# A transformer block on one core: an Exp bias in place of a matmul row, an earlier projection, and the expert tables in one pass

## The chip, the core and the metric

The kernel runs on 1 core of a Trainium2 chip. TensorE (PE) multiplies, ScalarE (ACT) applies functions, VectorE (DVE) and GpSimd (POOL) do elementwise work, and SP only issues DMAs. Each engine has its own queue and executes it in order; they meet at semaphores. The metric is the device time of one execution in microseconds (us), lower is better.

## The reference

Two layers on x of shape (2, 1024, 256), each behind a layer norm without scale and with a residual add: attention, then a mixture of experts.

```python
x = x + attention(_layernorm(x), wq, wk, wv, wo)
x = x + ffn(_layernorm(x), w_router, wg, wu, wd, sg, su, sd)
# attention: 32 heads of 8 dims, 8 key/value heads
scores = einsum('bhqd,bhkd->bhqk', q, k) / sqrt(8)
amask  = where((j >= i - 128) & (j < i), -1e10, 0)   # a band below the diagonal is masked
out    = einsum('bhqk,bhkd->bqhd', softmax(scores + amask), v) @ wo
# ffn: 8 routed experts, the top 2 per token with normalized sigmoid weights, and 2 shared ones
out = sum_e comb[t, e] * (silu(xt @ wg[e].T) * (xt @ wu[e].T)) @ wd[e].T + shared experts
```

## The kernel before, in words

**The start** (PE's L1557 to L1590). x comes in as 4 chunks of 512 rows. DVE takes each row's statistics, ACT the root, DVE the normalized rows; PE turns them (`transpose_x`, L1535), ACT copies the turned halves to `x1T` (`xT1_out`, L849), PE projects to q, k and v. PE passes the time up to the first turn with idle transposes (`idle_turns`, L1542: 52, later 8). q and k are split into three bf16 parts (`parts`), go to DRAM and come back, laid one above the other, as `qst` and `kst` of the stack of a group (`load_stack`, L527 and L530, SP). Rows of constants and shifts lie in the same stacks, so that one matmul adds up all the products. A bound on the scores, from the largest norms, is computed on a 1x1 chain of DVE and ACT; its negative is spread by a 1-column matmul (L1590) to 128 partitions and written as the row `kst[0]` and `kst[64]` by DVE (L1106) and ACT (L907), so that each score comes out with the bound subtracted. If the bound is too large for that, a flag starts an exact pass over all scores; all engines load the flag and branch (PE at L1594). With these inputs the flag is 0.

**The attention loop.** 16 groups (2 batches x 8 key/value heads), each 29 Exps over score blocks of 128 keys x 1024 (queries and heads), one of them of 512. PE computes scores (`scores`, L1616) into three double banks, DVE merges the masked diagonal blocks (`merge_pair`, L1149), ACT takes Exp (L930, L941, L933) into `prob`, POOL masks (`mask_pair`, L759), PE sums values and denominators in units of 4 heads (`values`, L1663) into banks 6 and 7. The order on PE is written out by hand in `TURNS`, 14 turns of products and ended values. Meanwhile DVE splits the expert weights, and SP loads the next stacks. DVE copies the sums out (`acc_out`, L1137), SP stores them to `o_scr`. PE may start a stack only when the semaphore `st_in` has its count; a first share of 32 is added by SP itself (L545).

**Out of the loop.** The sums of a chunk of 512 rows are loaded (`load_sums`), DVE inverts the denominators (`invert`, 4 pieces) and multiplies (`normalize`), PE projects with wo (`project`, L1716), DVE adds to x (`new_rows`, L1221), takes the second layer norm (`layernorm`, L449 to L462, root on ACT), PE turns (`transpose_rows`, L1726), ACT copies to `x2T` (`x2_out`, L947), and DVE takes the low parts and a plain copy (`xT_copy`) for the router. For chunk 0 all this stands behind the loop, for chunks 1 to 3 between the steps of the shared experts.

**The shared experts.** 4 chunks of 10 steps: `shared_up` (L1765, 12 matmuls), silu on ACT, products on DVE, `shared_down` (L1778). Routing is computed on DVE between steps 24 to 37 (`routing`): `slot_rows`, `slot_values` and `place_rows` make one-hot tables, PE multiplies them (`slot_products`, L1752), which gives for each slot of the 40 routed tiles its token and weight, and `slot_table` makes index lists of them.

**The routed experts.** Up to 40 tiles of 128 slots. POOL gathers rows (`gather`, L799) and adds results to `out` (`add`, L809); its adds wait until SP has stored the rows of the shared part, the last of them behind the load of expert 1. DVE's scaled result (`y_out`, L1506) waits for a free buffer that POOL's add gives back (L814).

## Time and profile before

| | us |
|---|---|
| median of 3 runs | 952.74 |
| lowest, highest | 952.62, 954.16 |
| the profiled execution | 952.9 |
| its span | 951.2 |
| TensorE's mean granted clock in it | 0.983 of full |

Busy in the span: PE 896.4 us (94%), ACT 583.4 (61%), DVE 444.9 (47%), POOL 278.7 (29%). These are means over stages that differ: the start to about 57 us, the attention loop to about 494, the shared experts to about 709, the routed ones to the end. A stage has to be read by itself, by stretches and by the timeline.

### The profile page before, as it was taken

The page shows a single profiled execution, that of the slowest core. Times are in us where ns is not written, and L with a number is a line of the kernel's source. Part 1 is how long each engine was busy: PE and PEld are TensorE (multiplying, and loading weights), DVE is VectorE, ACT ScalarE, POOL GpSimd, SP SyncE. Part 2 cuts the span into 40 slices and gives each one's busy share as a digit, 9 for nine tenths or more (in the row PEclk, how much of TensorE's full clock was granted, in tenths as well). Part 3 has the DMA queues.
Part 4 walks back from the last instruction along what each step waited for, and adds up shares of the span by engine and source line. Part 5 has one row for each costly group of instructions (what it writes and reads, how often), then busy time and mean ns, then how long its engine had stood idle before and what let it go on. Part 6 is the DMA issues. An engine that isn't in the chain of part 4 may idle for free.

```text
span 951.2 us, 24249 instructions
## 1 busy us (share of the span) xinstructions
PE 896.4 (94%) x8221; PEld 570.8 (60%) x8222; DVE 444.9 (47%) x761; ACT 583.4 (61%) x733; POOL 278.7 (29%) x422
## 2 busy tenths in 40 slices
PE   9959999999999999999988999999999999999994
PEld 6513333333333333333346888888887888888883
DVE  7724433444444334444456777656653433434332
ACT  4769999999999999999972423332222222222221
POOL 4403333233233333333330000000012545445442
PEclk9969999999999999999997999999999999999998
DMA  5433445555544455532202207100027864564521
GB/s 178 130 112 103 162 157 206 206 199 196 175 149 159 154 206 206 204 93 90 55 22 66 67 18 238 45 1 23 1 81 256 265 209 98 156 180 127 150 35 22
DMA packets 41951, 123.67 MB, mean 130 GB/s; under 512 B 7608, under 2 KB 22968, under 8 KB 35760
## 3 DMA queue, kind: packets, MB, share of 16 engines
q1 hardware_dynamic: 31152, 110.35, 34.0%
q0 software_dynamic: 7008, 9.70, 5.7%
q10 hardware_dynamic: 3744, 3.02, 1.0%
q8 instruction: 25, 0.41, 0.2%
q14 instruction: 22, 0.18, 0.1%
HBM read 74.03 MB, written 49.02 MB: 129 GB/s over the span
## 4 chain that ended last, share of the span: by engine, by line
PE 78%; ACT 8%; DVE 6%; issue 5%; SPq 1%; DMA 1%; DVEq 0%; POOLq 0%; POOL 0%; ACTq 0%
PE ps L1663 18%; PE ps L1811 14%; PE ps L1616 13%; PE ps L1765 11%; ACT arena L930 7%; PE ps L1830 7%; PE ps L1778 5%; DVE ps L1149 3%; PE ps L1557 2%; PE ps L1821 2%; PE ps L1716 1%; PE ps L1542 1%; PE ps L1792 1%; PE ps L1752 1%; PE ps L1734 1%
## 5 line engine op out<-in xcount | busy, mean ns | idle before, releaser
L930 ACT ACTIVATE arena<-ps 128x1024 f32<-128x1024 f32 x336 | 317.0, 1044 | 6.9 <-PE ps L1616 6.9
L1663 PE MATMUL ps<-arena 128*32 128x256 f32 x4096 | 265.1, 385 | 0.1
L759 POOL TENSOR_SCALAR_AFFINE_SELECT arena<-arena 128x512 f32<-128x512 f32 x240 | 150.0, 638 | 302.3 <-ACT arena L941 203.1
L1616 PE MATMUL ps<-arena 64*128 64x512 bf16 (+1 forms) x1280 | 184.5, 343 | 21.5 <-SPq L545 7.7
L1663 PEld LDWEIGHTS ps<-arena 128*32 128x32 f32 x4096 | 111.8, 109 | 103.1 <-issue 38.2
L1149 DVE COPY_PREDICATED ps<-keep,ps 128x512 f32<-128x512 int32 (+1 forms) x128 | 80.5, 629 | 172.1 <-PE ps L1616 172.1
L1616 PEld LDWEIGHTS ps<-arena 64*128 64x128 bf16 x1280 | 53.7, 94 | 175.4 <-ACT arena L930 82.2
L1811 PE MATMUL ps<-wr_all,x2T 128*128 x648 | 144.9, 364 | 5.7 <-issue 3.6
L1811 PEld LDWEIGHTS ps<-wr_all,x2T 128*128 128x128 f32 x648 | 105.6, 189 | 28.0 <-issue 13.7
L1765 PE MATMUL ps<-x2T,wr_all 128*128 128x512 f32 x480 | 118.8, 399 | 1.2 <-issue 1.2
L941 ACT ACTIVATE arena<-ps 128x1024 f32<-128x1024 f32 x112 | 114.2, 1034 | 8.0 <-DVE ps L1149 3.6
L1765 PEld LDWEIGHTS ps<-x2T,wr_all 128*128 128x128 f32 x480 | 89.5, 192 | 19.1 <-issue 1.6
L978 ACT CAST x2T<-ps 128x640 fp32r<-128x640 f32 x36 | 25.0, 693 | 107.4 <-PE ps L1821 101.4
L791 POOL COPY now_from<-slot_from 128x1 int32 (+1 forms) x36 | 10.1, 281 | 246.7 <-issue 232.0
L956 ACT ACTIVATE arena<-ps 128x512 f32<-128x512 f32 x40 | 23.9, 597 | 83.4 <-PE ps L1765 83.2
L1830 PE MATMUL ps<-wr_all,x2T 128*128 x540 | 73.3, 288 | 1.7 <-DVE x2T L1498 1.7
L809 POOL DMA_INDIRECT out<-arena,now_to x36 | 57.2, 1589 | 58.6 <-issue 46.9
L1830 PEld LDWEIGHTS ps<-wr_all,x2T 128*128 128x128 f32 x540 | 66.8, 191 | 2.1 <-issue 2.1
L983 ACT ACTIVATE arena<-ps 128x640 f32<-128x640 f32 x36 | 25.3, 704 | 64.1 <-PE ps L1811 62.3
L1778 PE MATMUL ps<-wr_all,hsh 128*128 128x256 f32 x480 | 64.1, 285 | 0.2 <-DVE hsh L1267 0.2
L1778 PEld LDWEIGHTS ps<-wr_all,hsh 128*128 128x128 f32 x480 | 61.8, 191 | 2.9 <-DVE hsh L1267 0.6
L1156 DVE CAST wr_all<-raw 128x1280 fp32r<-128x1280 f32 x30 | 24.7, 824 | 69.8 <-POOL arena L759 69.8
(187 smaller groups left out, 731.6 us busy)
## 6 DMA issues: line engine op xcount, KB each, us to landing
w_scr<-wr_all SPq DMA_DIRECT2D x24, 1280.0 KB, 7.0
wr_all<-w_scr SPq DMA_DIRECT2D x24, 1280.0 KB, 5.6
raw<-w_experts SPq DMA_DIRECT2D x24, 640.0 KB, 7.1
arena<-q_scr SPq DMA_DIRECT2D x64, 64.0 KB
o_scr<-arena SPq DMA_DIRECT2D x128, 32.0 KB, 1.6
arena<-o_scr SPq DMA_DIRECT2D x16, 256.0 KB, 3.9
raw<-w_shared SPq DMA_DIRECT2D x6, 640.0 KB, 4.2
q_scr<-parts SPq DMA_DIRECT2D x8, 384.0 KB, 2.8
```

Of the source, the lines that this page charges most:

```text
L759: nc.gpsimd.affine_select(out=dst, in_=src, compare_op=ALU.is_ge if own else ALU.is_gt, fill=0.0, base=0, pattern=[[0, REP], [-1 if own el ...
L809: nc.gpsimd.indirect_dma_start(out=out, in_=ysb[:, p, :], in_offset=None, compute_op=ALU.add, out_offset=bass.IndirectOffsetOnAxis(ap=now_ ...
L930: nc.scalar.activation(prob[:, SLOT[unit(a, kt)], :, :].rearrange("p h q -> p (h q)"), score.rearrange("p b x -> p (b x)"), ACT.Exp, scale ...
L941: nc.scalar.activation(halves, score.rearrange("p b (h s q) -> p (b h) s q", h=2, s=2), ACT.Exp, scale=SCALE).then_inc(s_free, 1)
L983: nc.scalar.activation(gact[:, p, :], ps[:, 0:3, :].rearrange("p b n -> p (b n)")[:, 0:I], ACT.Silu) \
L1149: nc.vector.copy_predicated(into, mask, source).then_inc(merged, 1)
L1616: return nc.tensor.matmul(ps[:, bank, :].rearrange("p (h q) -> p h q", h=2)[:, :, place * P:(place + tiles) * P], kst[r0:r0 + HALF, s, kt ...
L1663: last = nc.tensor.matmul(ps[32 * h:32 * h + 32, 6 + qc, a % 2 * QW:(a % 2 + 1) * QW], vst[:, s, kt, :], prob[:, SLOT[k], h, :], start=(no ...
L1765: last = nc.tensor.matmul(ps[:, 2 * (q % 2) + half, :], wr_all[:, q // KI, k, w, o:o + P], x2T[:, v, k, ds(c * CT, CT)], start=(k == 0 and ...
L1778: last = nc.tensor.matmul(ps[:, 4 + t // 2, t % 2 * D:(t % 2 + 1) * D], hsh[:, q % HR, v, t * P:(t + 1) * P], wr_all[:, q // KI, 2, w, o:o ...
L1811: last = nc.tensor.matmul(ps[:, n0 // 512, 0:n], xsT[:, p, v, k, :], wr_all[:, ds(slot, 1), k, w, n0:n0 + n].rearrange("p o n -> p (o n)") ...
L1830: last = nc.tensor.matmul(ps[:, 6, 0:D], hidT[:, p, v, k, :], wr_all[:, ds(slot, 1), 2, w, k * D:(k + 1) * D].rearrange("p o n -> p (o n)" ...
```

## The change

- The bound is copied by ACT to a [128, 1] tile `bound` and given to all Exps as bias. The rows `kst[0]` and `kst[64]` stay constant, those of `qst` zero; both memsets move from DVE to POOL. The four copies at L1106 and L907 go. `st_in`'s first share is added at the beginning of SP's program.
- The start: 30 and 4 idle turns for 52 and 8, and the second half of chunk 0's `x1T` is copied by DVE.
- Chunk 0's chain is moved into the loop: its sums are loaded after group 10, three of the four inversions stand in groups 12 to 14, the fourth and the product in group 15. `project(0)` stands in two halves between the last scores, into banks that are free by then (`FIRST_O`), and the last nine units of values behind it. Adds and statistics follow on DVE (`add_first`, `first_rows`), the turned rows go to banks 4 and 5 (`XT_BANK`).
- The tables: all operands are rounded fp32r, so that a product is one pass. The weight goes in as two parts, 3 x 40 = 120 columns for 2 x 40. The one-hot positions lie over columns of `x2T` that chunks 0 and 1 have used. The passes stand in steps 36 and 37 for 35 and 37, `place_rows(1)` in step 35 for 36.

The diff, cut to its core:

```diff
-EXP_STEP, RANK_STEP, TABLE_STEPS = 23, 27, (35, 37)
+EXP_STEP, RANK_STEP, TABLE_STEPS = 23, 27, (36, 37)
+HOT = 3
...
             sp.sem_inc(w_split, 2)
+            for s in range(2):
+                sp.sem_inc(st_in[s], 32)
...
             load_stack(1, 1)
-            for s in range(2):
-                sp.sem_inc(st_in[s], 32)
...
-            sp.wait_ge(o_stored[0], 16 * REP * KV + FIRST)
-            load_sums(0)
-            group_io(NG - 1, 1, False, False, False)
-            for c in range(1, NC):
+            for n in range(2 * LOOPED, NG - 1):
+                group_io(n, n % 2, n < SPLIT_PAIRS, n + 1 < NG - 1, n + 2 < NG)
+                if n == 2 * LOOPED:
+                    sp.wait_ge(o_stored[0], 16 * REP * KV + FIRST)
+                    load_sums(0)
+            store_acc(NG - 1, 0)
+            sp.wait_ge(o_stored[1], 16 * REP * KV + FIRST)
+            sp.wait_ge(c_proj, 2 + FIRST)
+            load_sums(1)
+            store_acc(NG - 1, 1)
+            for c in range(2, NC):
...
-                for k in range(KD):
+                for k in range(KD if c else 1):
                     nc.scalar.copy(x1T[:, c % 2, k, :], ps[:, k, :]).then_inc(a_xT, 1)
...
-            for s in range(2):
-                nc.scalar.copy(kst[HALF:HALF + 1, s, :], ps[HALF:HALF + 1, 7, 128:129].to_broadcast([1, L])) \
-                    .then_inc(shift_high, 1)
+            nc.scalar.copy(bound, ps[:, 7, 128:129]).then_inc(bound_ready, 1)
+            act.wait_ge(bound_ready, 1)
...
                         nc.scalar.activation(prob[:, SLOT[unit(a, kt)], :, :].rearrange("p h q -> p (h q)"),
-                                             score.rearrange("p b x -> p (b x)"), ACT.Exp, scale=SCALE).then_inc(s_free, 1)
+                                             score.rearrange("p b x -> p (b x)"), ACT.Exp, bias=bound, scale=SCALE).then_inc(s_free, 1)
...
+            def add_first(half):
+
+                dve.wait_ge(c_proj, half + 1 + FIRST)
+                for t in range(2 * half, 2 * half + 2):
+                    nc.vector.tensor_tensor(x_rows(0, t), x_rows(0, t), ps[:, FIRST_O[half], t % 2 * D:(t % 2 + 1) * D],
+                                            ALU.add) \
+                        .then_inc(c_added, 1)
+                for t in range(2 * half, 2 * half + 2):
+                    dve.wait_ge(c_added, t + 1)
+                    nc.vector.bn_stats(stats[:, t, :], x_rows(0, t)).then_inc(dve_step, 1)
...
             merge_pair(NG - 1, 1)
-            invert(0, 0)
-            invert(0, 1)
+            invert(0, INVERT - 1)
+            normalize(0)
             merge_pair(NG - 1, 2)
             acc_out(NG - 1, 0)
             merge_pair(NG - 1, 3)
-            invert(0, 2)
-            invert(0, 3)
-            normalize(0)
+            add_first(0)
+            add_first(1)
+            first_rows()
             acc_out(NG - 1, 1)
-            new_rows(0)
             xT_copy(0)
...
-                link(nc.vector.tensor_tensor(hot[:, :, 0, :], hot[:, :, 1, :], over_tiles(token_less_T[:, :], NTILE), ALU.mult))
-                nc.vector.tensor_tensor(hot[:, :, 1, :], hot[:, :, 1, :], over_tiles(w, NTILE), ALU.mult).then_inc(r_hot, 1)
+                nc.vector.tensor_tensor(hot[:, :, 0, :], one, over_tiles(token_less_T[:, :], NTILE), ALU.mult)
+                link(nc.vector.tensor_tensor(hot[:, :, 2, :], one, over_tiles(w_parts[:, k, 1, :].bitcast(F32), NTILE), ALU.mult))
+                nc.vector.tensor_tensor(hot[:, :, 1, :], one, over_tiles(w_parts[:, k, 0, :].bitcast(F32), NTILE), ALU.mult) \
+                    .then_inc(r_hot, 1)
...
-            idle_turns(7, 52)
+            idle_turns(7, 30)
             transpose_x(0)
-            idle_turns(7, 8)
+            idle_turns(7, 4)
...
+            products_of(*last, LAST_MERGE + 2, False)
+            pe.wait_ge(c_oT, 1)
+            pe.wait_ge(merged, NG * NMERGE)
+            project(0, range(0, 2))
+            products_of(*last, LAST_MERGE + 3, False)
+            pe.wait_ge(s_free, NG * NEXP - 2 + BUFS)
+            project(0, range(2, 4))
...
-                    last = nc.tensor.matmul(ps[:, 6, 0:2 * NTILE], pos_hot[k][:, t, :],
+                    last = nc.tensor.matmul(ps[:, 6, 0:HOT * NTILE], pos_hot[k][:, t // TPC, t % TPC, :],
...
-            project(0)
+            pe.wait_ge(s_free, NG * NEXP + BUFS)
             transpose_rows(0)
```

The order on two engines, at the two places that matter most. First ACT between the end of the start and the first Exps of the loop; before, with `ps` the scores and `arena` the memory in which `kst`, `prob` and the 1x1 values lie:

```order
L901 ACTIVATE arena<-arena 1x1 [waits u_top]
L904 ACT_TABLE_LOAD [waits ones_ready]
L904 ACTIVATE exp_of_one<-arena 1x1 [waits const]
L907 CAST arena<-ps 1x1024 [waits u_shift]
L907 CAST arena<-ps 1x1024
L930 ACTIVATE arena<-ps 128x1024 [waits s_ready,p_free] x7
L941 ACTIVATE arena<-ps 128x4x2x128 [waits merged,p_free]
```

and after:

```order
L913 ACTIVATE arena<-arena 1x1 [waits u_top]
L916 ACT_TABLE_LOAD [waits ones_ready]
L916 ACTIVATE exp_of_one<-arena 1x1 [waits const]
L918 COPY arena<-ps 128x1 [waits u_shift]
L941 ACTIVATE arena<-ps,arena 128x1024 [waits bound_ready,s_ready,p_free]
L941 ACTIVATE arena<-ps,arena 128x1024 [waits s_ready,p_free] x6
L952 ACTIVATE arena<-ps,arena 128x4x2x128 [waits merged,p_free]
L944 ACTIVATE arena<-ps,arena 128x4x128 [waits s_ready,p_free]
```

The two copies of 1x1024 have become one of 128x1, and each Exp (now L941, L952, L944) reads `arena` beside `ps`: the [128, 1] bound.

Then PE from the last scores to the turning of chunk 0's rows (L1616, now L1647, are scores; L1663, now L1694, values; L1716, now L1742, the projection; L1726, now L1772, the turns). Before, with the first of the six units of values that stand in between:

```order
L1616 MATMUL ps<-arena 128x512 [waits s_free]
L1616 MATMUL ps<-arena 128x512
L1663 MATMUL ps<-arena 32x256 [waits s_free]
L1663 MATMUL ps<-arena 32x256 x3
...
L1716 MATMUL ps<-wo_sb,arena 128x256 [waits c_lsb,c_oT,acc_free]
L1716 MATMUL ps<-wo_sb,arena 128x256 x3
L1716 MATMUL ps<-wo_sb,arena 128x256 [waits acc_free]
L1716 MATMUL ps<-wo_sb,arena 128x256 x3
L1726 MATMUL ps<-ident,arena 128x128 [waits c_xn]
L1726 MATMUL ps<-ident,arena 128x128 x7
```

and after, without the last eight units:

```order
L1647 MATMUL ps<-arena 128x512 [waits s_free]
L1647 MATMUL ps<-arena 128x512
L1742 MATMUL ps<-wo_sb,arena 128x256 [waits merged,c_oT]
L1742 MATMUL ps<-wo_sb,arena 128x256 x3
L1647 MATMUL ps<-arena 128x512 [waits s_free]
L1647 MATMUL ps<-arena 128x512
L1742 MATMUL ps<-wo_sb,arena 128x256 [waits s_free]
L1742 MATMUL ps<-wo_sb,arena 128x256 x3
L1694 MATMUL ps<-arena 32x256 [waits masked,s_free]
L1694 MATMUL ps<-arena 32x256 x3
...
L1772 MATMUL ps<-ident,arena 128x128 [waits c_xn,s_free]
L1772 MATMUL ps<-ident,arena 128x128 x7
```

The projection has moved ahead of the last scores and of the last nine units of values, half of it behind the third-last Exp, and the turns come straight after the values.

## Rows read from the trace of the kernel before

**Rows 1.** Stretches, two groups of the loop: busy us (instructions) per engine, clock, DMA

```profile
195.00:249.00 54.00, 52.33 (x672) 20.50 (x668) 21.86 (x30) 52.93 (x59) 18.65 (x30) 1.00 0.52 182
```

**Rows 2.** Costliest groups, the Exps: count | busy us, mean ns | idle before, releaser

```profile
L930 ACT ACTIVATE arena<-ps 128x1024 f32<-128x1024 f32 x336 | 317.0, 1044 | 6.9 <-PE ps L1616 6.9
L941 ACT ACTIVATE arena<-ps 128x1024 f32<-128x1024 f32 x112 | 114.2, 1034 | 8.0 <-DVE ps L1149 3.6 <-PE ps L1663 1.0
```

**Rows 3.** Timeline, twelve Exps in a row on ACT: start, us, what

```profile
217.33 11.24 ACT L930 ACTIVATE arena<-ps 128x1024 f32<-128x1024 f32 x12
```

**Rows 4.** Groups by shape on DVE, the last one on ACT: with and without [128,1] operands

```profile
L1506 DVE TENSOR_SCALAR arena<-ps,slot_w 128x256 f32<-128x256 f32 x36 | 17.4, 484 | 21.0 <-POOLq L814 11.1 <-issue 4.8 <-PE ps L1830 2.9
...
L1275 DVE TENSOR_TENSOR xres<-xres,ps 128x256 f32<-128x256 f32 x16 | 5.7, 416 | 4.0 <-PE ps L1778 4.0
...
L1034 DVE TENSOR_SCALAR arena<-xres,meanvar,rstd 128x256 f32<-128x256 f32 x16 | 5.6, 414 | 0.1
...
L1131 DVE COPY arena<-arena 128x256 f32 x10 | 2.9, 287 | 0.0
...
L1027 DVE TENSOR_SCALAR rstd<-meanvar 128x4 f32<-128x4 f32 x4 | 0.7, 170 | 0.1
...
L844 ACT ACTIVATE rstd<-rstd 128x4 f32<-128x4 f32 x8 | 1.7, 207 | 17.7 <-DVE rstd L456 16.0 <-DVE rstd L1027 1.6
```

**Rows 5.** Timeline, DVE: four and two of these in a row

```profile
12.39 1.38 DVE L1034 TENSOR_SCALAR arena<-xres,meanvar,rstd 128x256 f32<-128x256 f32 x4
...
52.06 0.47 DVE L1131 COPY arena<-arena 128x256 f32<-128x256 f32 x2
```

**Rows 6.** Timeline of the start; the last row is of the DMA issues (us to landing)

```profile
3.56 0.57 ACTq L891 DMA_DIRECT2D wr_sb<-w_router  x1
...
9.89 1.04 PE L1535 MATMUL ps<-ident,arena 128*128 128x128 f32 x8
...
12.30 5.53 PE L1557 MATMUL ps<-arena 128*128 128x512 f32 x12 [0.50 <-ACT arena L849]
...
wr_sb<-w_router ACTq DMA_DIRECT2D x1, 8.0 KB, 7.4
```

**Rows 7.** PE's branch on the flag (ns, start us); timeline, its first scores

```profile
L1594 PEldq COMPARE_BRANCH  x1: 365/365/365, 50.3 to 50.3; - x1
...
57.49 1.47 PE L1616 MATMUL ps<-arena 64*128 64x512 bf16 x6 [7.74 <-SPq L545]
```

**Rows 8.** Timeline out of the loop; the last row is a stretch with its clock

```profile
489.80 2.88 ACT L930 ACTIVATE arena<-ps 128x1024 f32<-128x1024 f32 x3
...
491.31 2.87 PE L1663 MATMUL ps<-arena 128*32 128x256 f32 x48
...
494.11 3.72 PE L1716 MATMUL ps<-wo_sb,arena 128*128 128x256 f32 x16
...
498.80 1.41 DVE L449 BATCH_NORM_STATS2 stats<-xres 128x6 f32<-128x256 f32 x4 [0.17 <-DVE xres L1221]
...
502.66 1.97 PE L1726 MATMUL ps<-ident,arena 128*128 128x128 f32 x8 [4.83 <-DVE arena L462]
...
505.84 5.46 PE L1765 MATMUL ps<-x2T,wr_all 128*128 128x512 f32 x12 [1.21 <-issue]
...
520.22 2.91 PE L1765 MATMUL ps<-x2T,wr_all 128*128 128x512 f32 x12
...
508.00:510.00 2.00, 2.00 (x6) 1.52 (x6) 1.86 (x2) 0.00 (x0) 0.00 (x0) 0.50 0.00 0
```

**Rows 9.** Timeline, tables and first weighed result; the last row is a DVE group

```profile
679.19 3.77 PE L1752 MATMUL ps<-arena,xres 128*128 128x80 f32 x32 [1.68 <-issue]
...
687.84 0.69 DVE L1264 TENSOR_TENSOR arena<-arena,ps 128x512 f32<-128x512 f32 x1 [3.61 <-ACT arena L956]
...
730.94 0.48 DVE L1506 TENSOR_SCALAR arena<-ps,slot_w 128x256 f32<-128x256 f32 x1 [2.93 <-POOLq L814]
...
L1427 DVE TENSOR_TENSOR arena<-arena,per_t 128x640 f32<-128x640 f32 x2 | 1.7, 826 | 0.1
```

More of the change, by code:

```diff
@@ L1170, in split_part, with group @@
                     split(n, p, lambda p: (w_staged[:, p, 0, :], w_staged[:, p, 1, :]), None)
-            def group(g, s, more):
+            def group(g, s, more, also=lambda: None):
                 merge_pair(g, 1)
+                also()
                 merge_pair(g, 2)
@@ L1193, in _ @@
                     group(it * 2 + s, s, True)
-            for n in range(2 * LOOPED, NG - 1):
-                group(n, n % 2, n + 2 < NG)
             def x_rows(c, t):
@@ L1666, in values, with products_of @@
                 last.then_inc(p_free, 1)
-            def turn_of(n, s, turn, t, before, after):
-                products, ended = TURNS[t]
-                for p in products:
+            def products_of(n, s, turn, t, after):
+                for p in TURNS[t][0]:
                     if not isinstance(p, int):
@@ L1720, in project @@
                         last.then_inc(c_proj, 1)
+            LAST_MERGE = max(t for t, (products, _) in enumerate(TURNS) if (QP - 1, 1) in products)
+            last = (NG - 1, 1, NG // 2 - 1)
+            for t in range(1, LAST_MERGE + 2):
+                turn_of(*last, t, True, False)
+            products_of(*last, LAST_MERGE + 2, False)
[5 more added lines that the diff above has]
+            project(0, range(2, 4))
+            for t in range(LAST_MERGE + 2, len(TURNS)):
+                if t > LAST_MERGE + 3:
+                    products_of(*last, t, False)
+                values_of(*last, t, True)
+            for v in TURNS[0][1]:
+                if len(v) == 3:
+                    values(NG - 1, 1, unit(*v[0:2]))
             def transpose_rows(c):
                 pe.wait_ge(c_xn, c + 1)
+                rows = xnc if c else xnc_first
                 for k in range(KD):
                     for t in range(TPC):
-                        last = nc.tensor.transpose(ps[:, 6 + k, t * P:(t + 1) * P], xnc[:, t, k * P:(k + 1) * P],
+                        last = nc.tensor.transpose(ps[:, XT_BANK[c] + k, t * P:(t + 1) * P], rows[:, t, k * P:(k + 1) * P],
                                                    ident[:, :])
```

143 lines of the change are left out of this document (74 added, 69 removed).

## The prediction

> **What bounds the kernel now.** I read the table of stretches first. In the attention loop, here two of its 16 groups, ACT is busy 52.93 of 54 us and PE 52.33 [rows 1]. Both look full, but PE's ends are modelled. The costliest groups of instructions tell them apart: the loop is 336 + 112 Exps of 1024 columns, of about 1.04 us each, and 16 of half that length [rows 2]. Twelve in a row take 11.24 us, so one starts every (11.24 - 1.04) / 11 = 0.927 us [rows 3]. A group has 29 Exps and takes 27.1 us; 28 x 0.93 + 0.5 is 26.5. So ACT sets the loop's pace, with about 1.07 / 2 = 0.53 us of idle per group. What lengthens an Exp lengthens the kernel, 464 times over.
>
> Three places outside the loop are bound by order, not by work: the entry into the loop, where PE stands for 7.74 us on a mere semaphore instruction of SP [rows 7]; the way out of it, where PE has nothing from 497.8 to 502.7 and the shared experts then start at half clock [rows 8]; and the tables of the routed tiles, where DVE waits 3.61 us [rows 9]. The change works on all three, and it touches every Exp.
>
> **The Exps' bias.** The constant -bound used to come into the scores as a row of the matmul; ACT's Exp now reads it as a [128,1] operand from SBUF. The second ordered list shows it: `arena<-ps` has become `arena<-ps,arena`. No ACT row of before has such an operand, so I bound its cost from DVE's rows, the nearest. With one such operand a 128x256 operation from PSUM takes 484 ns (L1506), without 416 (L1275): +68. With two, from SBUF, 414 (L1034), against 287 for a plain copy of that size (L1131): +127, or 63 each [rows 4]. Does it hide behind the instruction before? Four of L1034 take 1.38 us, one start every (1.38 - 0.414) / 3 = 0.322 us; two copies take 0.47, a start every 0.183 [rows 5]. The difference, 0.139 for two operands, is as large as in the durations: on DVE nothing hides. 68 ns are 0.40 of a 4-element operation of DVE (170 ns, L1027); 0.40 of ACT's (207 ns, L844 of ACT) is 83 ns [rows 4]. I take 83: 464 x 0.083 = **38.5 us**. Ends: 0, if ACT fetches it while the Exp before still streams, and 0.1 (half of ACT's 207), 46 us. A longer Exp leaves PE and DVE more time, so part of the 0.53 us of idle per group goes; I take half, 16 x 0.27 = 4.3 us (ends 0 and 8). Net **+34.2**.
>
> A rule speaks against this edit. The Trainium skill ("ScalarE: Activation LUTs", section "What ACT_TABLE_LOAD costs") gives an ACTIVATE with immediates 186 ns + 0.833 ns per element, about 93 ns more for each [128,1] operand, and an overlap of about 93 ns between neighbours. Its 1039 ns for 1024 columns agrees with the 1044 of the trace; no row here shows the 93. By it the forecast would be 464 x 0.010 = 4.6 us longer, 973.6.
>
> **The start, -1.0.** DVE's two large memsets go to POOL, which stood idle there and is through long before SP needs the constants at 33; 22 of the 52 idle turns go; the second copy of the first turned rows goes to DVE beside ACT's. The transposes, at 9.89 behind the idle turns, can come earlier, and so can the first projection at 12.30. But that also needs the last of the weights, issued at 3.56 and landing 7.4 later, at 10.96 [rows 6]. So at most 1.3; I take 1.0, at least 0.5. The cover that could go is PE's clock: with fewer idle turns it may be granted half for the 12 projection matmuls, 3 us worse.
>
> **Into the loop, -6.4.** PE waits for st_in, which SP raises in its queue only behind the whole load of the second stack; the first matmul runs at 57.49 [rows 7]. The change raises it at SP's beginning. Next in line is PE's own branch on the flag, which ends at 50.3 + 0.37 = 50.67 [rows 7], 49.7 with the earlier start. The bias is one 128x1 copy on ACT, beside PE's first scores, in place of four 1x1024 copies, so it is not late. With 0.4 for the code behind the jump the first scores come at 50.1, 7.4 earlier than 57.49: 1.0 is the start's and 6.4 are this edit's. If that code is fetched late, 5. The second stack, issued by 56, is used a group later.
>
> **Out of the loop, -8.8.** Call T the end of the last Exp, 489.80 + 2.88 = 492.68. Before: values to T + 1.5, projection 3.72, adds, statistics, layer norm, transposes at T + 10.0, first shared matmul at T + 13.2; its 12 matmuls take 5.46 at clock 0.50 (1.2 GHz) and 2.91 at full [rows 8]. The clock was 1.00 up to the 4.8 us in which PE had no matmul (the idle before the transposes), and 0.50 behind them. Now inversion and product move between the merges of groups 12 to 15, where DVE waits anyway. The first half of the projection runs between the last scores, the second as soon as the third-last Exp is done. It ends about T + 0.1. DVE adds and takes the statistics by T + 1.8; from the end of the statistics to the transposes it took 502.66 - (498.80 + 1.41) = 2.45 [rows 8], so c_xn comes at T + 4.2. PE meanwhile has nine units of values, 9 x 0.48 = 4.3 (six take 2.87, rows 8), which now stand behind the projection. So: values to T + 4.5, transposes to T + 5.8 and ACT's two copies to T + 7.1, then the shared matmuls, at full clock since PE is hardly idle: done at T + 10.0, where before it was T + 18.6. That is 8.6, and 0.2 for the router, which was partly slow too. If the clock falls all the same it is 6. What queues behind PE's new waits is the last nine values; their output is not needed before the next chunk. On SP the four loads of the first sums move up behind group 10, ahead of group 11's stores and loads, and those of the second sums ahead of the last store; both queues have a whole group of time there.
>
> **The tables, -1.8.** Two passes of 3.77 us on PE become one-pass products: 16 of about 0.1 us each. PE saves some 4 us and 2 of waits, but that isn't the gain. The index is ready when DVE is through. It loses its wait of 3.61 us, since the second positions now follow at once, and gains two 128x640 operations of 0.826 (L1427) and one small of 0.22 [rows 9]: 3.61 - 1.65 - 0.22 = 1.75. Everything behind hangs on the index, not on PE: the first gathers, then expert 1's load, the last row store, POOL's first add, and then DVE's y_out, which waited 2.93 us for it until 730.94 [rows 9]. PE will wait there for what it gained. Ends: 1.0 and, if that chain is looser than I read it, 4.
>
> **Sum**, against the profiled 952.9, which stands 0.2 over the median 952.74: 34.2 - 1.0 - 6.4 - 8.8 - 1.8 = +16.2, so **969.0** on the median.
>
> **The rivals.**
> - *The operand is free.* ACT reads it while the Exp before streams. Then 952.7 - 18.0 = 934.7, and 0.4 for an Exp of the last group that waits behind the half projection on PE: 935.1; with the ends above, 931 to 942. For it: ACT's neighbours overlap, 1044 ns long at a spacing of 927 [rows 2, 3]. Against: DVE's overlap too, and there the operand's time stays. It decides the sign: below (18.0 + 4.3) / 464 = 0.048 us per Exp the change is faster, or 0.039 if no idle is absorbed.
> - *Half hidden*, 40 ns: 18.6 - 4.3 - 18.0 = -3.7, 949; 944 to 956.
> - *The way out gains little.* The half projection holds up the last Exps, or c_xn waits, or the clock is lost: 3 to 5 less gained, 973.5.
>
> **How the numbers follow.** A measurement tells about 0.2%, 1.9 us. Forecast 0.51 (own range 957 to 981); way out worse as well 0.09; operand free 0.31; half hidden 0.07; rest 0.02, slower. Faster: 0.31 and 0.04 of the half hidden, 0.35. Same 0.02. Slower 0.63. Both signs hold much, so the range takes in both groups: 932.5 to 981.
>
> **What would show it.** Right or wrong at once: the Exps' mean in the changed profile, 1.12 us at a spacing of 1.01, and a group of 29.3 us; if the spacing stays at 0.93, the first rival holds. The first scores at 50; no wait of PE for SP. After the last Exp, first shared matmul at T + 7 with clock 1.00. DVE without its 3.6 us of wait in the tables, PE with a new wait of about 2 us before the first routed transpose. Wrong would be: more Exp idle than 0.5 us per group, a clock of 0.50 in the first 20 us, or more than a few tenths of idle on PE before the second half of the projection.

## The result: slower, as forecast, by other terms than forecast

The changed kernel takes **968.77 us** (median of 4 runs, 966.48 to 971.54), the kernel before beside it 953.34 (4 runs, 952.62 to 954.16): a ratio of 1.0163, 95% interval 1.0134 to 1.0191. The forecast was 969.0. The profiled execution took 968.79 us with a span of 967.1; that of before, 952.9 and 951.2. The difference of the spans, 15.9 us, is what is taken apart here.

The Exps of the changed kernel, from the costliest groups (busy us, mean ns, idle before), and five in a row from ScalarE's timeline (start us, us). They answer to [rows 2, 3]:

```profile
L941 ACT ACTIVATE arena<-ps,arena 128x1024 f32<-128x1024 f32 x336 | 348.7, 1192 | 1.4 <-PE ps L1647 1.4
L952 ACT ACTIVATE arena<-ps,arena 128x1024 f32<-128x1024 f32 x112 | 123.9, 1168 | 0.6 <-PE ps L1647 0.3 <-DVE ps L1160 0.3
L944 ACT ACTIVATE arena<-ps,arena 128x512 f32<-128x512 f32 x16 | 13.2, 822 | 0.0
```

```profile
53.73 6.14 ACT L941 ACTIVATE arena<-ps,arena 128x1024 f32<-128x1024 f32 x6 [1.22 <-PE ps L1647]
...
509.44 5.17 ACT L941 ACTIVATE arena<-ps,arena 128x1024 f32<-128x1024 f32 x5
```

An Exp is 148 ns longer than the 1044 of [rows 2]. The spacing is what the loop pays: (5.17 - 1.19) / 4 = 0.995 us, where it was 0.927 [rows 3]. The idle ahead of the Exps is nearly gone.

The way out of the loop, TensorE's timeline; it answers to [rows 8]:

```profile
510.96 2.00 PE L1742 MATMUL ps<-wo_sb,arena 128*128 128x256 f32 x8
512.89 0.39 PE L1647 MATMUL ps<-arena 64*128 64x512 bf16 x2
513.21 1.99 PE L1742 MATMUL ps<-wo_sb,arena 128*128 128x256 f32 x8
515.13 4.09 PE L1694 MATMUL ps<-arena 128*32 128x256 f32 x72
519.20 1.06 PE L1772 MATMUL ps<-ident,arena 128*128 128x128 f32 x8
521.48 3.41 PE L1811 MATMUL ps<-x2T,wr_all 128*128 128x512 f32 x12 [1.21 <-issue]
```

The last Exp ends at 509.44 + 5.17 = 514.61. The first shared matmul starts 6.87 us behind it, the last of the twelve ends at + 10.3, and they run at full clock (3.41 us, 5.46 before).

The tables and the first routed transpose, TensorE's timeline; they answer to [rows 9]:

```profile
694.74 1.90 PE L1798 MATMUL ps<-tile_hot,x2T 128*128 128x120 f32 x16
701.17 2.00 PE L1798 MATMUL ps<-tile_hot,x2T 128*128 128x120 f32 x16 [0.30 <-DVE x2T L1468]
714.96 0.41 PE L1838 MATMUL ps<-ident,xres 128*128 128x128 f32 x2 [1.94 <-issue]
```

**Five stretches of each profile.** The program is cut at four marks that all kernels have: the start of the first Exp, the end of the last, TensorE's first and last transpose of gathered rows in the routed stage. In us, read from the timelines:

```
                            first Exp  Exps   to first   to last   to the   span
                            starts at         routed T.  routed T. end
before                        58.20   434.49   212.95     221.46   24.10   951.2
after                         53.73   460.88   200.35     226.77   25.37   967.1
after less before             -4.47   +26.39   -12.60      +5.31   +1.27   +15.9
before + operand              58.57   460.32   212.06     222.01   24.14   977.1
after, immediate bias         53.65   435.40   200.54     226.38   24.13   940.1
after, no band mask           52.85   461.57   200.27     226.74   24.07   965.5
both (base, below)            51.05   435.81   200.53     226.47   24.14   938.0
  same, again                 50.86   436.03   200.58     226.52   25.51   939.5
base, 60 idle turns           50.57   435.69   200.56     227.97   25.31   940.1
  same, again                 51.12   435.70   200.50     228.49   25.29   941.1
before, 34 idle turns         57.33   435.70   212.74     222.09   24.14   952.0
base, four passes             52.83   434.93   201.47     223.19   24.28   936.7
base, projection last         50.75   435.27   208.03     226.54   24.11   944.7
base, loads apart             50.78   435.17   200.53     225.83   24.09   936.4
base, loads apart, 60         51.45   435.77   200.44     225.77   25.77   939.2
```

Most runs below move the stretch that they edit and hardly any other, which is what makes the table readable. The routed stretch ("to last") is the exception: it moves in the runs with 60 turns and with four passes, which don't touch it, and these moves are taken up below.

### The profile page after: what moved, and what is told of

Same layout as the page of the kernel before. It is cut to its first block, busy times and chain, and to the rows that moved or that the text cites. A ratio compares the mean times of both kernels' runs of the same rounds, so it can differ in the third digit from the quotient of the medians.

```text
span 967.1 us, 24131 instructions
## 1 busy us (share of the span) xinstructions
PE 897.2 (93%) x8163; PEld 564.7 (58%) x8164; DVE 447.1 (46%) x765; ACT 615.5 (64%) x731; POOL 277.1 (29%) x422
## 4 chain that ended last, share of the span: by engine, by line
PE 62%; ACT 18%; issue 8%; DVE 7%; DMA 3%; POOLq 1%; POOL 0%; DVEq 0%; ACTq 0%; SPq 0%
ACT arena L941 13%; PE ps L1694 13%; PE ps L1857 12%; PE ps L1647 11%; PE ps L1811 8%; PE ps L1876 6%; PE ps L1824 4%; ACT arena L952 2%; PE ps L1867 2%; PE ps L1589 2%; DMA wr_all<-w_scr 2%; PE ps L1742 1%; DVE ps L1160 1%; ACT arena L944 1%; DVE hsh L1298 1%
## 5 line engine op out<-in xcount | busy, mean ns | idle before, releaser
L941 ACT ACTIVATE arena<-ps,arena 128x1024 f32<-128x1024 f32 x336 | 348.7, 1192 | 1.4 <-PE ps L1647 1.4
L1694 PE MATMUL ps<-arena 128*32 128x256 f32 x4096 | 264.7, 385 | 0.8 <-POOL arena L771 0.8
L1647 PE MATMUL ps<-arena 64*128 64x512 bf16 (+1 forms) x1280 | 190.5, 343 | 32.5 <-ACT arena L941 22.1
L1647 PEld LDWEIGHTS ps<-arena 64*128 64x128 bf16 x1280 | 55.0, 94 | 199.0 <-ACT arena L941 101.8
L1694 PEld LDWEIGHTS ps<-arena 128*32 128x32 f32 x4096 | 112.1, 109 | 97.3 <-issue 36.5
L952 ACT ACTIVATE arena<-ps,arena 128x1024 f32<-128x1024 f32 x112 | 123.9, 1168 | 0.6 <-PE ps L1647 0.3
L1811 PE MATMUL ps<-x2T,wr_all 128*128 128x512 f32 x480 | 116.7, 393 | 1.3 <-issue 1.2
L1530 DVE TENSOR_TENSOR x2T<-ps,x2T 128x640 fp32r<-128x640 f32 x36 | 29.7, 824 | 62.7 <-ACT x2T L990 62.7
```

What stands on the lines that cost most here:

```text
L941: nc.scalar.activation(prob[:, SLOT[unit(a, kt)], :, :].rearrange("p h q -> p (h q)"), score.rearrange("p b x -> p (b x)"), ACT.Exp, bias= ...
L952: nc.scalar.activation(halves, score.rearrange("p b (h s q) -> p (b h) s q", h=2, s=2), ACT.Exp, bias=bound, scale=SCALE).then_inc(s_free, 1)
L1530: nc.vector.tensor_tensor(hidT[:, p, 1].rearrange("p k t -> p (k t)"), ps[:, 4:6, :].rearrange("p b n -> p (b n)")[:, 0:I], hidT[:, p, 0]. ...
L1647: return nc.tensor.matmul(ps[:, bank, :].rearrange("p (h q) -> p h q", h=2)[:, :, place * P:(place + tiles) * P], kst[r0:r0 + HALF, s, kt ...
L1694: last = nc.tensor.matmul(ps[32 * h:32 * h + 32, 6 + qc, a % 2 * QW:(a % 2 + 1) * QW], vst[:, s, kt, :], prob[:, SLOT[k], h, :], start=(no ...
L1811: last = nc.tensor.matmul(ps[:, 2 * (q % 2) + half, :], wr_all[:, q // KI, k, w, o:o + P], x2T[:, v, k, ds(c * CT, CT)], start=(k == 0 and ...
```

## The experiments

### The operand, taken out and put in

After, with the bias taken out of the Exps:

```
-  ACT.Exp, bias=bound, scale=SCALE)
+  ACT.Exp, scale=SCALE)
```

> The changed kernel with the bias operand taken out of the attention's Exps (all 464 of the loop), nothing else: the bound is still computed and copied, no Exp reads it, and the softmax is the same without it. Theory A, the operand costs on ScalarE's path what the two traces show from the first Exp to the end of the last (434.5 us before, 460.9 after, 26.4 us over 464 Exps, 0.057 each): this kernel ends near 968.8 - 26.4 = 942.4 us, and the mean of one Exp at 128x1024 goes back from 1192 ns to about 1044 ns. Theory B, the operand is mostly hidden behind the fixed part of the next Exp and the loop grew for another reason (the new order of the last pairs, the moved projection, the work that DVE has in the loop): the duration falls by some 148 ns but the spacing hardly, and the time stays above 960 us. Theory C, as the prediction had it, 0.083 each and 4.3 us given back by idle time: 934.6 us.

This kernel and all that are built on it leave out the subtraction of the bound: it is computed and then read by no Exp. They tell the price of the operand and are no replacement for it. Measured: 941.86 us (941.75 to 942.50), 0.9878 of before (0.9863 to 0.9893). Before, with a column of zeros as bias:

```
-  ACT.Exp, scale=SCALE)
+  ACT.Exp, bias=nothing, scale=SCALE)
```

> The kernel before with one thing added: each Exp of the attention takes a bias from a column of zeros in SBUF (128x1), set once at the start; the Exps compute the same. Two columns are set on GpSimd (the second is not read here). Theory A (the operand alone makes the loop longer): 953.3 + 26.4 = 979.7 us, first Exp to last +26 us. Theory B (the loop grew for another reason): within 8 us of 953.3. Theory C (the prediction's price, 0.083 us per Exp less 4.3 us of idle time): 953.3 + 34.2 = 987.5 us.

Measured: 978.77 us (976.84 to 979.27), 1.0258 (1.0243 to 1.0273). The same two groups, first with the immediate bias, then of before with the operand:

```profile
L941 ACT ACTIVATE arena<-ps 128x1024 f32<-128x1024 f32 x336 | 317.1, 1044 | 2.0 <-PE ps L1647 2.0
L952 ACT ACTIVATE arena<-ps 128x1024 f32<-128x1024 f32 x112 | 114.2, 1034 | 8.7 <-DVE ps L1160 4.2 <-PE ps L1694 1.0 <-PE ps L1647 0.7
```

```profile
L934 ACT ACTIVATE arena<-ps,nothing 128x1024 f32<-128x1024 f32 x336 | 348.8, 1193 | 6.6 <-PE ps L1620 6.6
L945 ACT ACTIVATE arena<-ps,nothing 128x1024 f32<-128x1024 f32 x112 | 124.3, 1173 | 0.2 <-DVE ps L1153 0.2
```

Theory A holds from both sides: the Exps' stretch is 434.5 to 436.0 us without the operand, 460.3 to 461.6 with it, whatever else the kernel has. The idle that went is 8.7 us (10.7 less the first wait of 1.2, against 2.0 less 1.2). So without its waits the loop is 460.9 - 0.8 = 460.1 and 435.4 - 9.5 = 425.9 us long, and one operand costs 34.2 / 464 = **0.074 us**. The other pair gives the same: before has 14.9 us of idle in these groups [rows 2] and before with the operand 6.8, each with a first wait of 6.06, so (25.8 + 8.1) / 464 = 0.073 us.

### The start: GpSimd's mask across DVE's subtraction

In the changed profile DVE and GpSimd meet at 32.9 us. Rows of DVE, GpSimd and ScalarE there:

```profile
32.90 1.79 POOL L756 TENSOR_SCALAR_AFFINE_SELECT arena<-arena 128x1920 f32<-128x1920 f32 x1
32.94 2.28 DVE L1065 TENSOR_TENSOR parts<-arena,parts 128x512 bf16<-128x512 f32 x1 [0.68 <-ACT parts L880]
...
35.86 0.62 ACT L880 CAST parts<-arena 128x512 bf16<-128x512 f32 x1 [1.80 <-DVE arena L1055]
```

The same meeting in the kernel before, where DVE was first by 0.02 us:

```profile
33.77 0.69 DVE L1055 TENSOR_TENSOR parts<-arena,parts 128x512 bf16<-128x512 f32 x1 [0.68 <-ACT parts L868]
33.79 2.32 POOL L744 TENSOR_SCALAR_AFFINE_SELECT arena<-arena 128x1920 f32<-128x1920 f32 x1
```

Who comes second pays: DVE 1.59 us, or GpSimd 0.53. The Trainium skill ("SBUF — State Buffer", section "SBUF: two separate sides") has a rule for it: a DVE operation with two SBUF inputs and a GpSimd operation that reads SBUF share a port pair, which the first to start holds to its end. The rows agree in kind: DVE's end, 35.22, is 0.53 us behind the selection's end at 34.69, and in before the selection's end, 36.11, is 1.65 us behind DVE's end at 34.46, each a little less than the operation takes undisturbed (0.69 and 1.79).

The shorter idle turns alone don't turn the order. The kernel before with the idle turns of after (a run of the section on the routed stage) has both operations as early as after, and DVE first again:

```profile
32.90 0.69 DVE L1055 TENSOR_TENSOR parts<-arena,parts 128x512 bf16<-128x512 f32 x1 [0.69 <-ACT parts L868]
32.92 2.33 POOL L744 TENSOR_SCALAR_AFFINE_SELECT arena<-arena 128x1920 f32<-128x1920 f32 x1
```

So something else in the change turns it. Candidates are DVE's copy of `x1T` and the memsets moved to GpSimd; no run takes these apart.

In the changed kernel TensorE then runs dry and its clock falls; stretches of the changed kernel (after the length: TensorE, its weight loads, DVE, ScalarE, GpSimd, then the granted clock):

```profile
36.00:40.00 4.00, 2.53 (x16) 1.66 (x15) 2.51 (x4) 3.22 (x7) 1.94 (x5) 0.86 0.24 74
40.00:44.00 4.00, 4.00 (x8) 1.54 (x6) 0.97 (x2) 1.23 (x3) 0.00 (x0) 0.72 0.61 200
```

So the mask was taken out (a part that this input never reads):

```
-  step(nc.gpsimd.memset(bandmask[:, :], MASKED))
-  step(nc.gpsimd.affine_select(out=bandmask[:, :], ...))
-  nc.gpsimd.affine_select(out=bandmask[:, :], ...).then_inc(band_ready, 1)
+  nc.gpsimd.memset(bandmask[:, 0:P], MASKED).then_inc(band_ready, 1)
```

> The changed kernel without GpSimd's band mask in the start (a memset and two selections over 128x1920 elements; only its first 128 columns are set, and the mask is read on the branch with the large bound alone, which this input does not take). Theory A, the start came out 2.3 us longer instead of 1.0 shorter because DVE's subtraction at 32.94 us (2.28 us instead of 0.69) stood behind GpSimd's selection that had started at 32.90, and TensorE went to half clock in the gap: without that work DVE's tile takes 0.7 us again, no half clock between 38 and 44 us, the bound's chain ends near 48 us instead of 51.2, and the time is 968.8 - 3 = 965.8 us. Theory B, the shorter idle turns or the early transposes brought the clock down: the half clock stays, and the time with it (968.8).

Measured: 964.96 us (964.20 to 967.26), 1.0116 (1.0100 to 1.0131). DVE's row is back at 0.69 us and the clock is 1.00 from 20 to 48 us, but the profile has lost 1.8 us in another place. Its stretches, and those of the run with both edits:

```profile
12.00:16.00 4.00, 4.00 (x6) 1.66 (x7) 2.13 (x6) 1.32 (x3) 2.16 (x1) 0.62 0.07 26
```

```profile
12.00:16.00 4.00, 4.00 (x10) 1.51 (x11) 3.09 (x10) 2.14 (x5) 1.96 (x1) 1.00 0.13 43
```

Half clock came in the first projections, which the prediction named as the cover that could go with the idle turns (at 3 us; it costs 1.8). It came in two of nine profiles with 34 turns (this one and the one with four passes) and in none of five with 60; whether the turns decide it, so few can't tell.

> The changed kernel without the bias operand and without GpSimd's band mask (both edits of the two runs beside it; the mask is read on a branch that this input does not take). If the two costs add, 968.8 - 26.4 - 3 = 939.4 us, some 14 us under the kernel before. If the start's loss is swallowed by the loop (ScalarE waits for the first scores anyway), it equals the run with the immediate bias alone, 942.4.

Measured: 940.93 us (939.68 to 941.52), 0.9868 (0.9853 to 0.9883). The first Exp starts at 51.05, where the forecast's own start and entry would put it at 58.2 - 7.4 = 50.8. In the spans it is 2.1 us less than with the immediate bias alone. The medians are 0.9 us apart, between the two forecasts, 939.4 and 942.4, so they don't settle whether the costs add. This kernel is the **base** of the rest.

### The way out

```
   products_of(*last, LAST_MERGE + 2, False)
-  pe.wait_ge(c_oT, 1)
-  pe.wait_ge(merged, NG * NMERGE)
-  project(0, range(0, 2))
   products_of(*last, LAST_MERGE + 3, False)
-  pe.wait_ge(s_free, NG * NEXP - 2 + BUFS)
-  project(0, range(2, 4))
   ...
           values(NG - 1, 1, unit(*v[0:2]))
+  pe.wait_ge(c_oT, 1)
+  pe.wait_ge(merged, NG * NMERGE)
+  project(0, range(0, 4))
```

> The kernel with the immediate bias and without the band mask, with the projection of the first tiles moved back behind the last values (the rest of the way out as changed: sums loaded and inverted early, banks, DVE's own order). TensorE then does the last values first and the projection after them, and DVE's additions, the layernorm and the transposes follow. Theory A, what the way out gained (the first shared product of the second step starts 12.6 us after the end of the last Exp where it stood 20.5 before, and the first routed transpose came 12.4 us nearer to the last Exp) is the projection's place: it comes back by the time from the first half's projection (3.7 us ahead of the last Exp's end) to the end of the values (some 5 us behind it), 8 us: 940.9 + 8 = 949 us. Theory B, the early loads and inversions made most of the gain and the place of the projection is worth only its own 4 us: 945 us.

Measured: 946.50 us (946.08 to 949.25), 0.9932 (0.9906 to 0.9957); 5.6 us over the base, 7.5 in its stretch. TensorE's timeline, and a stretch with the clock:

```profile
487.68 3.72 PE L1736 MATMUL ps<-wo_sb,arena 128*128 128x256 f32 x16
495.39 1.94 PE L1764 MATMUL ps<-ident,arena 128*128 128x128 f32 x8 [4.00 <-DVE arena L473]
498.54 5.46 PE L1803 MATMUL ps<-x2T,wr_all 128*128 128x512 f32 x12 [1.21 <-issue]
```

```profile
498.00:504.00 6.00, 5.46 (x14) 4.32 (x14) 4.01 (x3) 1.73 (x2) 0.00 (x0) 0.50 0.33 98
```

The last Exp ended at 486.02: the first shared matmul is at + 12.5 again, the last at + 18.0, with a wait of 4 us (4.83 in [rows 8]) and half clock as in [rows 8]. The early loads and inversions are worth 0.7 us without the projection's move; the move is worth the rest, of which 2.05 us are the clock. The stretch speaks for theory A's 8 us; the median lies between the two theories.

### The tables

The slot products of the base read as plain fp32:

```
-  pos_hot[k][...], tile_hot[k][...]
+  pos_hot[k][...].bitcast(F32), tile_hot[k][...].bitcast(F32)
```

> The kernel with the immediate bias and without the band mask, with the two slot passes of the tables read as plain fp32 (the tiles and the 120 columns unchanged): TensorE takes them in more passes, as in the kernel before, where 16 products of 80 columns took 3.77 us. For 120 columns that is 3.77 x 120 / 80 = 5.7 us for each pass over the tiles, against 1.9 to 2.0: 3.7 us more, twice. Theory A, the shared stage is bound by TensorE there, the first pass's 3.7 us count in full and the second's too, less the 1.9 us that TensorE waits ahead of the first routed transpose: 940.9 + 5.6 = 946.5 us. Theory B, the index chain on DVE and GpSimd sets the end and the passes lie beside other waits: within 2 us of 940.9.

Measured: 938.95 us (936.66 to 940.30), 0.9842 (0.9816 to 0.9869): theory B, and my price was wrong too:

```profile
668.12 3.73 PE L1792 MATMUL ps<-tile_hot,x2T 128*128 128x120 f32 x32
675.87 3.73 PE L1792 MATMUL ps<-tile_hot,x2T 128*128 128x120 f32 x32
```

120 columns take 3.73 us where 80 took 3.77 [rows 9]. Up to the first routed transpose the run is 0.94 us longer, of 3.5 us more work: TensorE gives back its wait of 1.97 us there, as the prediction had it. That the run isn't slower than the base lies in the next stretch, 3.3 us shorter; the section below takes that up.

### The routed stage, which nobody had touched

It came out 5.3 us longer. Ahead of the same six products, once in each round of TensorE's loop (two tiles), stands a gap. One row of before and one of after:

```profile
781.69 0.98 PE L1811 MATMUL ps<-wr_all,x2T 128*128 x6 [0.17 <-issue]
```

```profile
794.53 0.97 PE L1857 MATMUL ps<-wr_all,x2T 128*128 x6 [0.36 <-issue]
```

"Issue" means that nothing in the profile is waited for. In the program two loads of slot numbers into TensorE's registers stand there. The groups over the same 172 us of the loop, of before and of after:

```profile
L1811 PE MATMUL ps<-wr_all,x2T 128*128 x496 | 111.5, 365 | 2.2 <-issue 2.2
```

```profile
L1857 PE MATMUL ps<-wr_all,x2T 128*128 x487 | 109.3, 364 | 4.9 <-issue 4.9
```

That is 2.7 us of the 5.3. The change removed 26 idle turns ahead of that loop, so I asked whether it hangs on where the program lies.

```
-  idle_turns(7, 30)   ...   idle_turns(7, 4)
+  idle_turns(7, 52)   ...   idle_turns(7, 8)
```

> The kernel with the immediate bias and without the band mask, with the idle turns at TensorE's start put back to 52 and 8 (60 instead of 34, as before the change). Two questions. The start: the first real transposes then come at 9.9 us instead of 8.4 and the first projection near 12.3 instead of 11.5, so the first Exp comes some 0.8 us later than 51.05 if TensorE's beginning sets the start, and at the same time if DVE and ScalarE do. The routed stage: between the first routed transpose and the last the changed kernel and all its variants take 226.4 to 226.8 us, the kernel before and its variant with the operand 221.5 to 222.0, with a gap of 0.36 to 0.39 us instead of 0.16 to 0.19 us in each of 17 rounds of the loop, before the six products that follow two loads of slot numbers into registers. Theory P, the gap hangs on where TensorE's program lies: the change took 26 instructions out ahead of that loop, and with them back the gap is 0.18 again and the stage 3 us shorter (some 223 us; time 940.9 - 3.2 + 0.8 = 938.5 us). Theory Q, it comes of something else (the phase of the other engines, data placed elsewhere): the stage stays at 226.5 and the time at 941 to 942 us.

> The kernel before with nothing changed but the idle turns: 30 and 4 instead of 52 and 8. Start: the first transposes at 8.4 us, the first projection at 11.5 (0.8 earlier), the first scores 0.8 us earlier than 57.49 at most. Theory P (the gap in the routed loop hangs on where TensorE's program lies): 26 instructions fewer stand ahead of the loop as in the changed kernel, the gap goes from 0.18 to 0.37 us in 17 rounds and the stretch from the first routed transpose to the last from 221.5 to some 224.7; time 953.3 + 3.2 - 0.8 = 955.7 us. Theory Q: the stretch stays at 221.5 to 222 and the time is 952.5 to 953.3 us.

Measured: the base with 60 turns 941.23 us (938.13 to 943.16), 0.9859 (0.9836 to 0.9882), its gap 0.16 to 0.21; before with 34 turns 953.62 us (952.18 to 957.24), 0.9997 (0.9981 to 1.0012), its gap still 0.17 to 0.21. The first gap speaks for P, the second against it, and the run with four passes, with the base's turns, has 0.15 to 0.21. (These are the steady rounds; the first and last two of the loop differ.)

With 60 turns the shorter gap doesn't make the stretch shorter. Theory P's 223 us and 938.5 didn't come: the stretch is 227.97, the longest so far. At the fifth tile TensorE waits for a gather and runs at half clock behind it (15 products that take 2.04 us elsewhere take 3.56):

```profile
712.56 0.97 PE L1851 MATMUL ps<-wr_all,x2T 128*128 x6 [0.17 <-issue]
715.99 0.65 PE L1832 MATMUL ps<-ident,xres 128*128 128x128 f32 x2 [2.46 <-DMA xres<-xn_scr,now_from]
717.33 3.56 PE L1870 MATMUL ps<-wr_all,x2T 128*128 x15 [0.68 <-DVE x2T L1524]
```

In the base the same wait is 0.20 us. This gather stands in GpSimd's program behind the wait for SP's last row store, which SP issues when expert 1's weights are in. From the first of these loads to the store it is 16.69 us in the base and 18.04 with 60 turns; why the loads take longer there is open. So only the run with four passes shows what the gap costs: TensorE's idle by "issue" is 3.2 us less than the base's and the stretch 3.3 us shorter.

The first question of that run, on the start, has an answer too. The first projection comes at 11.56 us and the first Exp at 50.57, no later than the base's 11.89 and 51.05 (the second profiles of both: 12.09 and 51.12 against 11.69 and 50.86). In the changed kernel the 26 turns taken out bring nothing: in the base TensorE waits 2.05 us for DVE's copy of `x1T` before the first projection.

Is the gap chance? The two were profiled again:

> The same kernel as the one with the immediate bias and without the band mask, profiled a second time. It asks whether two things that came out differently among the variants are fixed in a program or fall out anew in each execution. The gap ahead of the six products behind the two loads of slot numbers was 0.36 to 0.39 us in each round of the routed loop there, and 0.16 to 0.19 in the variant with 60 idle turns and in the one with four passes: fixed in the program, it is 0.37 again and the stretch between the first and the last routed transpose 226.5 us; a state of the execution, it can come out at 0.18 and 223 us. The clock in the first projections (12 to 16 us) was at full there and at half in two other variants with the same start: a state of the execution, it may be at half this time and the first Exp at 52.85 instead of 51.05 us.

> The same kernel as the variant with 60 idle turns (immediate bias, no band mask), profiled a second time, for the same question. Fixed in the program: the gap in the routed loop is 0.18 us again. A state of the execution: it can be 0.37 us. With 60 idle turns I expect full clock from 12 to 16 us and the first Exp near 50.6 us both times.

Measured: 940.02 (2 runs) and 940.39 us (2 runs), 0.9847 (0.9814 to 0.9881) and 0.9851 (0.9812 to 0.9890), and the gaps as before, 0.35 to 0.41 and 0.17 to 0.21 in the steady rounds. So the gap is, by two profiles of each, fixed in a program. The gather's wait with 60 turns came again too (2.75 us, the stretch 228.49; 0.25 us in the base). What falls out anew is the end, 24.14 us in one profile of the base and 25.51 in the other: in the ten us from 20 to 10 before the end the granted clock is 1.00 in the first and 0.83 in the second. It is 1.00 there in before and 0.83 in after, so that after's +1.27 is likely of that kind.

Last, the place of the loads, on both:

```
-  slot_1, (slot_0, slot_2) = routed_rest(j, 0, lambda: slot_tile(j + 1), i + 1,
-                                         lambda: (slot_tile(j), slot_tile(j + 2)))
+  slot_1, slot_0 = routed_rest(j, 0, lambda: slot_tile(j + 1), i + 1, lambda: slot_tile(j))
+  slot_2 = slot_tile(j + 2)
   routed_down(j, 0, slot_0)
```

> The kernel with the immediate bias and without the band mask, with one edit in TensorE's routed loop: of the two loads of slot numbers into registers that stood one behind the other between the first and the second piece of a tile's products, the second moves ahead of that tile's down products. Theory A, the gap in each round (0.37 us there) is the two loads outlasting the 1.64 us of products that cover them: with one load in each place both are covered, the gap goes, 17 x 0.37 = 6.3 us, 940.9 - 6.3 = 934.6 us, and the stretch from the first routed transpose to the last goes from 226.5 to some 220.5 us. Theory B, TensorE's sequencer needs the time wherever the loads stand: the gap moves ahead of the down products and the time stays at 940.9.

> The same edit as in the run beside it (the second load of a slot number ahead of the down products) on the variant with 60 idle turns, immediate bias and no band mask; it is the fastest version that the reasons so far point to. Theory A: no gap in the loop here either, so that the stretch from the first routed transpose to the last is as long as in the run beside it (220.5 us) though the gaps had been 0.37 there and 0.18 here; time 941.2 - 17 x 0.18 = 938 us or less, 934 if the late transposes of its last profile were a chance. Theory B: as before the edit, 941 us.

Measured: 939.86 us (937.29 to 940.84), 0.9843 (0.9819 to 0.9867); and 938.37 us (935.16 to 940.92), 0.9826 (0.9799 to 0.9853). In the first the gap has moved to where the load now stands:

```profile
779.68 2.05 PE L1870 MATMUL ps<-wr_all,x2T 128*128 x15 [0.32 <-issue]
792.34 2.05 PE L1870 MATMUL ps<-wr_all,x2T 128*128 x15 [0.29 <-issue]
```

In the second it is gone from most rounds. So the loads make the gap (it follows them), but theory A's 6.3 us aren't there: only 0.1 per round is won on the base. The second keeps the wait for the fifth tile's gather (2.27 us), and its stretch is 225.77, not 220.5. This last kernel has the lowest median of all, 1.7% under before (it too leaves out the bound's subtraction and the mask), but its lead over the base and over the run with four passes is within their spread.

**What stays open** is why one program's loads take 0.2 us longer than another's. One reading fits every profile: TensorE records a plain fp32 slot product as two instructions (x32 in the rows of before and of the four passes, x16 after), so the change took out 26 + 32 = 58 ahead of the loop; the six profiles that lack all 58, with the loads where they were, have the long gap, and those that lack none, 26 or 32 have the short one. I found that count afterwards; no run tested it, by filling up the 58 with other instructions, for example.

The rest of the stretch's 5.3 us, some 2.6, lies for the most part in the first rounds. At the fifth tile TensorE waits 0.55 us for the gather and then 0.97 for DVE; before has neither wait. (It has the 1.85 us for DVE at the second tile, as after does, so that one explains nothing.) And the granted clock is 0.83 in the 10 us from 724.96, where before has 1.00 in the first 20. The lead of the transposes over the rest of the chain had shrunk: from before to after they came 12.6 us nearer to the last Exp, the index, by DVE's last table operation (698.68 before, 709.89 after), 10.7, and SP's last row store, for which the fifth gather waits (722.09, 734.07), 9.9. That the waits come of this lead is argued from the distances; no run takes it alone.

## The prediction, step by step

**The Exp operand, +34.2: right in sign, 8 us too high, and the price in part by luck.** The net is 26.4 from before to after. The price, 83 ns taken over from DVE's rows, measured 74, so that 38.5 becomes 34.2. The idle absorbed was 8.7 and not 4.3; half of the idle was my choice, and all but 0.8 us went. That leaves 25.5, the difference between the changed kernel with and without the operand; the other 0.9 of the 26.4 is there without the operand too (435.40 against 434.49). The price stands over the break-even of 48 ns, and that settled the sign. But the mechanism behind it, "on DVE nothing hides", isn't ScalarE's. The duration grew by 148 ns (200 at 512 columns) and not by 83, the spacing by 68, and 80 between were hidden and not nothing: two errors that nearly cancel. I had forecast a mean of 1.12 us at a spacing of 1.01; it is 1.19 at 0.995. By the duration alone, 464 x 0.148, the loop would have grown by 69 us. The rivals *operand is free* and *half hidden* fall.

The Trainium skill ("ScalarE: Activation LUTs", section "What ACT_TABLE_LOAD costs") gives 93 ns more for each [128,1] operand and an overlap of 93 ns between neighbours. Neither is this case's figure: the duration grew by 148 ns, and the overlap, duration less spacing, grew with it from 117 to 197 ns. Its 973.6 us is 4.8 over the measured time.

**The start, -1.0: it came out at +2.3.** The first half of the step is right: transposes at 8.37, the first projection at 11.47 instead of 12.30. But TensorE waits 1.57 us ahead of it for DVE's copy, and the kernel with 60 turns starts no later; before with 34 turns, whose copies are both ScalarE's, gets there at 11.42. The step that failed is "the cover that could go is PE's clock": I looked for it behind the idle turns alone. In the profile it went 25 us later, behind DVE's subtraction, ahead of which GpSimd's mask had started by 0.04 us; the prediction moved work to DVE and GpSimd in the start and priced no meeting of the two. The bound's last operation on DVE started at 51.24 instead of 48.98. Without the mask, when the clock holds, the matmul that spreads the bound comes at 48.77 and 48.56 for 49.17 before: 0.4 to 0.6 us gained, near the forecast's low end of 0.5.

**Into the loop, -6.4: right.** The first scores come at 53.02, 4.47 earlier; against the start's 2.26 later that is 6.7, with no wait for SP.

**The way out, -8.8: right, and for the reason given.** With T again the end of the last Exp: T + 6.87 for the first shared matmul (T + 7.1), full clock, T + 10.3 for its end (T + 10.0). The second step of the shared experts, which began at T + 20.5 before, begins at T + 11.8: 8.7 won. The projection's place does it and the early loads alone bring 0.7 us, as the run with the projection last shows.

**The tables, -1.8: right, 2.0 by the index**, with 1.94 us of wait on TensorE as announced. But "everything hangs on the index, not on PE" was half right: the routed transposes came 1.9 us nearer to the last Exp than it did, and TensorE waited 1.5 us at the fifth tile instead, behind its gather.

**The routed stage, 0: +4.7** (5.3 and 1.3 of the table, less the 1.9 that the transposes had run ahead). No step of the prediction spoke of it. The instructions there are the same. Of the 6.6 us before that is taken off, 2.7 are a gap that is fixed in a program and whose cause stays open, and 1.5 the waits at the fifth tile; the other 2.4 fall where the profile shows spells of half clock that before doesn't have.

The sum: +26.4 + 2.3 - 6.7 - 8.7 - 2.0 + 4.7 = +16.0 against +16.2. The forecast time was met because an Exp term 8 us too high stood against a start and a routed stage 8 us too low. The direction was earned, by the count of Exps and a price above the break-even; that the time agrees to 0.2 us is luck.

## What to carry to other kernels

A per-partition operand on an instruction that sets the pace costs its price times the count: 74 ns here, 464 times, more than all that the rest of the change won (11.8 us by the medians). Before moving a constant out of a matmul row (the first six score matmuls take 1.47 us with the bound in it and without) into a [128,1] operand of the pacing engine, measure the spacing, not the duration, with and without it. And a change that moves work between engines can flip which of two reaches a shared resource first: here DVE was first by 0.02 us before, and GpSimd by 0.04 after. Last, a stretch that nobody edited can move by 5 us, and a shorter gap in it need not shorten it: compare whole stretches, over several programs.

## What was not expected of the hardware

- ScalarE, Exp from PSUM, bias as an SBUF column: the duration 1044 to 1192 ns (1024 columns), 622 to 822 (512), the spacing 0.927 to 0.995 us.
- A DVE subtraction of 0.69 us took 2.28 when a GpSimd selection over SBUF had started 0.04 us ahead of it; with the order turned, GpSimd's took 2.32 instead of 1.79.
- 16 plain fp32 products with 128x128 weights take 3.77 us at 80 columns and 3.73 at 120; rounded, in one pass, 1.90 to 2.00.
- Two loads into TensorE's registers leave a gap of 0.17 or 0.37 us in the stream of matmuls, the same in each execution of a program and different between programs with the same loop.
